# A graph network whose tables hold the layers' inputs instead of their products

## The chip, the cores and the metric

The kernel runs on one core of a Trainium2 chip. The metric is the time of the device for one execution, in microseconds (us). Before the change three runs took 3906.57, 3909.14 and 3911.62 us.

Five engines work side by side: TensorE (PE in the rows: matrix products, and turns, which are products with the identity), VectorE (DVE), ScalarE (ACT), GpSimd (POOL, which issues the indirect transfers) and SyncE (SP, which issues the plain ones).

## The reference

Four graph stages follow one another over 50,000 nodes of 128 features and 25,000 edges sorted by target, each as x = layernorm(x + stage(x)). The stage that matters here is the second, a graph convolution of three layers:

```python
deg = segment_sum(1, dst) + 1            # a loop at every node
norm = deg[src] ** -0.5 * deg[dst] ** -0.5
h = x @ W_in + b_in
for i in range(3):
    xw = h @ Ws[i]
    agg = segment_sum(xw[src] * norm, dst) + bs[i]
    h = relu(agg)
```

The stage ahead of it (attention with four heads, gelu, layernorm) gives x1; after it comes x2 = layernorm(x1 + h), then two more attention stages. A product with Ws[i] and the weighted sum over edges can be exchanged: sum of (h @ W) is (sum of h) @ W.

## The kernel before

The work is in stages, each a block in which every engine has its own written instruction list; semaphores order them, and all engines meet between the stages.

- *Node stage.* All nodes are computed as if they had no edge: 49 iterations over 1024 rows each (two halves of 512), with the layernorms of iteration t-1, t-2, t-5, t-6 and t-7 in one batch on VectorE (forty columns: big, half_y, hx, wx, then rs and nm). For a chunk m = t-3, TensorE turns x1 (into the PSUM banks T_A and T_B), makes h1 = W_in Ws0 applied to it (with the feature on the partition), and beside it the same product with the node on the partition (rows_times), which are the rows of the first table, xw0; the same again with Ws1 for h2 and table xw1, and with Ws2 for table xw2. VectorE adds the bias to xw0 (L793), ScalarE copies xw1 and xw2 out of PSUM (L658, L677, L689, L703), and VectorE reads the copy of xw2 for h3 (L741) and v (L746). SyncE stores the three tables, x2 and x3. Meanwhile GpSimd gathers x at the ends of the edges and writes a map of nodes that are targets.
- *First hop.* The attention stage for the targets of edges, 25 iterations of 1024 edge slots. VectorE forms the batch of scales up to nm (L1485), ScalarE normalises (L1377) and then normalises again to x1 (L1389); TensorE turns x1, ScalarE copies (L1363), TensorE multiplies by W_in Ws0 on top of a bias row (L1308, L1310), ScalarE scales the rows by deg^-0.5 (L1349), and SyncE stores them in the first table.
- *Graph layers 0, 1 and 2.* Each 49 chunks of 512 slots. GpSimd gathers four times 128 rows of the layer's table (L1607), up to six chunks ahead; SyncE loads the slots' own rows. TensorE turns both; VectorE first adds the bias times root(deg) to the own rows (L1709, four instructions), then runs a segmented sum over the gathered columns (the scan, L1714) and adds the own column (L1721, with_self). ScalarE applies relu (hT, L1653); TensorE multiplies by the next layer's matrix and ScalarE scales (L1661) to the rows of the next table. In layer 2 TensorE only turns hT back and VectorE makes v = x1 + deg^-0.5 h from PSUM (L1758, four instructions), followed by a layernorm. Beside them a part of the final layernorms of all nodes (y) and turns of the edge features run.
- *The last two hops* follow from 2585 us on; their order comes from a table of places. The change doesn't touch them.

## Time and profile before

| | |
|---|---|
| median of three runs | 3909.14 us |
| the profiled execution | 3892.84 us, span 3891.1 us |
| VectorE busy | 3381.2 us (87%) |
| TensorE busy | 2681.5 us (69%) |
| ScalarE busy | 2534.8 us (65%) |
| GpSimd busy | 2446.9 us (63%) |

The span is the time from the first to the last instruction in the profile. The shares are means over stages with different limits, so that each stage has to be read by itself. A busy time counts the union of an engine's instructions; on VectorE they overlap by about a tenth of a microsecond where nothing waits, so a duration and the distance of two starts are not the same. In brackets behind an instruction of a timeline stands how long the engine was idle ahead of it, and what ended that. The granted clock is TensorE's, as a share of 2.4 GHz; its low level is 1.2 GHz.

### The profile page before, as it was taken

What the parts mean: (1) busy time and instruction counts of PE and PEld (TensorE: products, weight loads), DVE (VectorE), ACT (ScalarE), POOL (GpSimd) and SP (SyncE); (2) the same over time, 40 slices, a digit from 0 to 9 for tenths busy, and PEclk for the clock granted to TensorE, in tenths of its full rate; (3) what the DMA queues carried; (4) which work ended last, traced back from release to release, by engine and by line L of the source; (5) the groups of instructions that cost most, each with busy time, mean ns of one, the idle gap of its engine ahead of it and who ended that gap; (6) DMA issues with size and microseconds to landing.
All of it is one profiled execution on the core that took longest, in us unless ns stands there. A gap on an engine that the chain in (4) does not pass through costs nothing. (4 is left out here: it accounts for less than half of the span.)

```text
span 3891.1 us, 48029 instructions
## 1 busy us (share of the span) xinstructions
PE 2681.5 (69%) x11826; PEld 1733.3 (45%) x11826; DVE 3381.2 (87%) x7569; ACT 2534.8 (65%) x5535; POOL 2446.9 (63%) x2202
## 2 busy tenths in 40 slices
PE   5877877778861688865656545547888885776774
PEld 4555555555540344435545534424444442444442
DVE  5999999999987788858868869969999996998886
ACT  3788788878862466645646646637777775565554
POOL 4565566666650566517767767757766651788777
PEclk9999999999985677767676775659999887666555
DMA  3888877766652988837868868832333221433332
GB/s 102 195 197 199 199 197 199 199 197 194 203 177 79 252 253 258 253 110 239 270 196 257 261 203 252 248 122 81 90 86 87 83 77 52 112 96 92 95 95 65
DMA packets 402066, 644.05 MB, mean 166 GB/s; under 512 B 127455, under 2 KB 207720, under 8 KB 401790
## 3 DMA queue, kind: packets, MB, share of 16 engines
q1 hardware_dynamic: 332030, 527.96, 45.1%
q0 software_dynamic: 69760, 113.02, 11.9%
q8 instruction: 99, 1.62, 0.2%
q14 instruction: 177, 1.45, 0.1%
HBM read 347.78 MB, written 296.81 MB: 166 GB/s over the span
## 5 line engine op out<-in xcount | busy, mean ns | idle before, releaser
L1607 POOL DMA_INDIRECT gs_g<-table_xw,slot_idx x588 | 612.2, 1041 | 297.7 <-issue 257.0
L898 POOL DMA_INDIRECT gs_t<-table_x,slot_idx x392 | 439.7, 1122 | 310.9 <-POOLq L83 125.4
L507 POOL DMA_INDIRECT gs<-x,src_idx x200 | 219.5, 1098 | 342.1 <-DMA xd_rows<-gd 249.3
L1274 POOL DMA_INDIRECT slot_idx<-node_map,src_idx x200 | 242.9, 1214 | 192.7 <-DMA slot_idx<-node_map,src_idx 91.7
L378 PE MATMUL ps<-ident,own_g 128*128 128x128 f32 x588 | 139.8, 382 | 251.5 <-DVE own_g L1709 251.2
L1653 ACT ACTIVATE hT_g<-u_g 128x512 f32<-128x512 f32 x147 | 92.5, 629 | 330.9 <-DVE u_g L1721 330.7
L507 POOL DMA_INDIRECT gd<-x,dst_idx x200 | 243.9, 1220 | 60.9 <-issue 59.1
L1883 POOL DMA_INDIRECT out<-x_t,end_idx x196 | 234.6, 1197 | 59.9 <-issue 59.0
L495 POOL DMA_INDIRECT node_map<-slot_no,end_idx x200 | 222.9, 1114 | 61.0 <-issue 60.6
L898 POOL DMA_INDIRECT own_t<-table_x,own_idx x196 | 222.2, 1134 | 59.7 <-issue 59.4
L1714 DVE TENSOR_TENSOR_SCAN agg_g<-same_seg,agg_g,ps 128x512 f32<-128x512 uint8 x147 | 187.3, 1274 | 48.5 <-PE ps L378 48.2
L1709 DVE SCALAR_TENSOR_TENSOR own_g<-bs_row,root,own_g 128x128 f32<-128x128 f32 x588 | 166.7, 345 | 67.5 <-DMA own_g<-table_xw 67.4
L378 PEld LDWEIGHTS ps<-ident,own_g 128*128 128x128 f32 x588 | 93.2, 192 | 290.8 <-DVE own_g L1709 290.5
L378 PE MATMUL ps<-ident,gs_g 128*128 128x128 f32 x588 | 130.6, 365 | 127.5 <-DMA gs_g<-table_xw,slot_idx 127.4
L611 ACT ACTIVATE x_b<-v_b,nm,rs 128x128 f32<-128x128 f32 x392 | 156.2, 480 | 68.8 <-DVE nm L785 68.8
L2000 ACT COPY xsT_t<-ps 128x512 f32<-128x512 f32 x98 | 56.4, 576 | 208.9 <-PE ps L378 208.9
L378 PE MATMUL ps<-ident,gs_t 128*128 128x128 f32 x392 | 81.4, 345 | 126.9 <-DMA gs_t<-table_x,slot_idx 99.7
L611 ACT ACTIVATE x_b<-s_b,nm,rs 128x128 f32<-128x128 f32 x392 | 156.3, 485 | 11.9 <-DVE nm L785 11.9
L378 PEld LDWEIGHTS ps<-ident,gs_g 128*128 128x128 f32 x588 | 99.2, 193 | 141.8 <-issue 88.9
L378 PEld LDWEIGHTS ps<-ident,gs_t 128*128 128x128 f32 x392 | 56.9, 176 | 236.4 <-issue 236.4
L384 PEld LDWEIGHTS ps<-WS,h1T 128*128 128x128 f32 x784 | 100.8, 194 | 137.4 <-DVE xw_b L793 112.3
L384 PE MATMUL ps<-WS,h1T 128*128 128x128 f32 x784 | 109.9, 284 | 74.4 <-DVE xw_b L793 74.4
(366 smaller groups left out, 9514.9 us busy)
## 6 DMA issues: line engine op xcount, KB each, us to landing
table_xw<-xw_b SPq DMA_DIRECT2D x147, 512.0 KB, 4.8
table_x<-x_b SPq DMA_DIRECT2D x98, 512.0 KB, 2.7
own_g<-table_xw SPq DMA_DIRECT2D x147, 256.0 KB, 4.3
x_in<-x SPq DMA_DIRECT2D x49, 512.0 KB
y_g<-table_x SPq DMA_DIRECT2D x49, 512.0 KB, 4.8
table_xw<-xw_g SPq DMA_DIRECT2D x98, 256.0 KB
out<-y_g SPq DMA_DIRECT2D x49, 512.0 KB, 3.6
pen_t<-pen_row SPq DMA_DIRECT2D x98, 256.0 KB, 4.0
```

The lines of the kernel that those rows point to most:

```text
L378: last = nc.tensor.transpose(to[0:width, j * P:(j + 1) * P], t[:, j * width:(j + 1) * width], ident[:])
L384: last = nc.tensor.matmul(to[:, j * D:(j + 1) * D], tT[:, j * P:(j + 1) * P], W[:], start=True, stop=bias_row is None)
L495: pool.indirect_dma_start(out=node_map, out_offset=bass.IndirectOffsetOnAxis(ap=end_idx[:, t:t + 1], axis=0), in_=slot_no[:, t:t + 1], in_ ...
L507: pool.indirect_dma_start(out=to[k % 3][:, j * D:(j + 1) * D], out_offset=None, in_=x, in_offset=bass.IndirectOffsetOnAxis(ap=of[:, n:n + ...
L611: last = nc.scalar.activation(to[:, k * D:(k + 1) * D], of(k), ACT.Identity, scale=r[:, n, k:k + 1], bias=b[:, n, k:k + 1])
L898: pool.indirect_dma_start(out=self.B[L % RING][g][:, t * D:(t + 1) * D], out_offset=None, in_=table, in_offset=bass.IndirectOffsetOnAxis(a ...
L1274: pool.indirect_dma_start(out=slot_idx[:, t:t + 1], out_offset=None, in_=node_map, in_offset=bass.IndirectOffsetOnAxis(ap=src_idx[:, t:t + ...
L1607: pool.indirect_dma_start(out=gs[c % 6][:, j * D:(j + 1) * D], out_offset=None, in_=tables[layer], in_offset=bass.IndirectOffsetOnAxis(ap= ...
L1653: nc.scalar.activation(hT[c % 3][:], u[c % 2][:], ACT.Relu).then_inc(S("hT"), 1)
L1709: V.scalar_tensor_tensor(out=blk, in0=bs_row[layer][:], scalar=root4[:, k:k + 1], in1=blk, op0=ALU.mult, op1=ALU.add).then_inc(S("own_bias ...
L1714: V.tensor_tensor_scan(agg[t % 3][:], same_seg[:, t * CH:(t + 1) * CH], T_X[t % 2], agg[(t - 1) % 3][:, CH - 1:CH], ALU.mult, ALU.add).the ...
L1883: pool.indirect_dma_start(out=out, out_offset=bass.IndirectOffsetOnAxis(ap=end_idx[:, k:k + 1], axis=0), in_=B[L % RING]["x4"][:, t * D:(t ...
```

## The change

The tables no longer hold products but the inputs of the layers: x1, h1 and h2 (with the factor deg^-0.5 for the edge slots), and each graph layer sums first and multiplies by its own matrix then. The order of a layer is: turn and scan, with_self, product with WS[layer] (z), bias times root(deg) added on VectorE (zb, four instructions, from PSUM), relu with the scale on ScalarE (h_e, four instructions), store. It runs one chunk deeper. In layer 2, v becomes one addition of 512 columns from SBUF, a chunk later than before.

The bias b_in Ws0 of the first layer is carried by x1 itself: x1 is a layernorm's output, whose features have the mean 0. Its shift nm is raised by 1.0 with one small VectorE instruction on 8 columns, so that the mean of x1 is 1; the matrix is centred (centre times W_in Ws0) and the bias, divided by 128, is added to each of its rows. The following layernorms take the constant out again.

In the node stage the row products with W_in Ws0 go, with VectorE's two bias additions; the row products with Ws1 become turns of h1, and turns of h2 are added, while the row products with Ws2 stay, for h3. VectorE reads h3 directly from PSUM, in two halves. In the first hop the turns of x1, their copies and the products go; the rows are x1 times deg^-0.5, by ScalarE, and the same small addition of 1.0 stands behind its nm. The diff below is cut; the second halves and the other waits read alike.

```diff
-    tables = [dram(f"table_{n}", [NT + rows, D]) for n, rows in (("xw0", ET), ("xw1", GT), ("xw2", GT), ("x2", GT), ("x3", GT))]
+    tables = [dram(f"table_{n}", [NT + rows, D]) for n, rows in (("x1", ET), ("h1", GT), ("h2", GT), ("x2", GT), ("x3", GT))]
...
+        pe.wait_ge(S("wi0"), 1)
+        pe.wait_ge(S("centre"), 1)
+        nc.tensor.matmul(ps[:, 4, 0:P], centre[:], WI[:], start=True, stop=True).then_inc(S("wi0_centred"), 1)
...
+        V.scalar_tensor_tensor(out=WS[0][:], in0=xw0_bias[:], scalar=1.0 / D, in1=ps[:, 4, 0:P], op0=ALU.mult, op1=ALU.add)
...
-                store(tables[0], xw_b[0], "xw0_out", 2, t - 3, "xw0", 2 * (t - 2))
-                store(tables[1], xw_b[1], "xw1_out", 2, t - 3, "xw1", 2 * (t - 2))
-            if live(t - 3):
-                store(tables[2], xw_b[2], "xw2_out", 2, t - 3, "xw2", 2 * (t - 2))
+                store(tables[0], x1_b, "x1_out", 3, t - 3, "b_out", 2 * (t - 2))
+                store(tables[1], h_b[1], "h1_out", 2, t - 3, "h1_rows", 2 * (t - 2))
+                store(tables[2], h_b[2], "h2_out", 2, t - 3, "h2_rows", 2 * (t - 2))
...
-                    pe.wait_ge(S("xw2"), 2 * c)
+                    pe.wait_ge(S("h3"), 2 * c)
                 turn(pe, T_A, half(x1_b[c % 3], 0)).then_inc(S("x1T_ps"), 1)
                 pe.wait_ge(S("b_out"), 2 * c + 2)
                 if c:
-                    pe.wait_ge(S("xw1"), 2 * c)
+                    pe.wait_ge(S("h2_rows"), 2 * c)
                 turn(pe, T_B, half(x1_b[c % 3], 1)).then_inc(S("x1T_ps"), 1)
                 pe.wait_ge(S("x1T"), 2 * c + 1)
-                nc.tensor.matmul(T_C, WI0[:], x1T[0][:], start=True, stop=True).then_inc(S("h1_ps"), 1)
-                rows_times(pe, T_D, x1T[0], WI0).then_inc(S("xw0_ps"), 1)
+                nc.tensor.matmul(T_C, WS[0][:], x1T[0][:], start=True, stop=True).then_inc(S("h1_ps"), 1)
...
             if m:
                 pe.wait_ge(S("h1T"), 2 * c + 1)
                 nc.tensor.matmul(T_C, WS[1][:], h1T[0][:], start=True, stop=True).then_inc(S("h2_ps"), 1)
-                pe.wait_ge(S("xw0"), 2 * c + 1)
-                rows_times(pe, T_D, h1T[0], WS[1]).then_inc(S("xw1_ps"), 1)
+                turn(pe, T_D, h1T[0]).then_inc(S("h1_turned"), 1)
...
                 pe.wait_ge(S("h2T"), 2 * c + 1)
                 rows_times(pe, T_C, h2T[0], WS[2]).then_inc(S("xw2_ps"), 1)
+                pe.wait_ge(S("h1_rows"), 2 * c + 1)
+                turn(pe, T_D, h2T[0]).then_inc(S("h2_turned"), 1)
             if f:
...
-                act.wait_ge(S("xw2_ps"), 2 * c + 1)
+                act.wait_ge(S("h2_turned"), 2 * c + 1)
                 if c >= 2:
-                    landed(act, "xw2_out", 2, c - 2)
-                    act.wait_ge(S("h3"), c - 1)
-                nc.scalar.copy(half(xw_b[2][c % 2], 0), T_C).then_inc(S("xw2"), 1)
+                    landed(act, "h2_out", 2, c - 2)
+                nc.scalar.copy(half(h_b[2][c % 2], 0), T_D).then_inc(S("h2_rows"), 1)
...
-                v.wait_ge(S("xw2"), 2 * (cv + 1))
-                V.tensor_tensor(wide_rows(h3_b[:]), wide_rows(xw_b[2][cv % 2][:]), row_of_all(bs_row[2]), ALU.add).then_inc(S("h3"), 1)
-            if live(cv):
-                v.wait_ge(S("h3"), cv + 1)
+                for h in range(2):
+                    v.wait_ge(S("xw2_ps"), 2 * cv + h + 1)
+                    V.tensor_tensor(rows4(half(h3_b, h)), rows4((T_C, T_A)[h]), each_row(bs_row[2]), ALU.add).then_inc(S("h3"), 1)
+                v.wait_ge(S("h3"), 2 * (cv + 1))
...
             v.wait_ge(S("batch"), n0 + 10)
-            V.scalar_tensor_tensor(out=b, in0=of[:, :, 1], scalar=-1.0, in1=r, op0=ALU.mult, op1=ALU.mult).then_inc(S("scaled"), 1)
-
-            m, c, a = live(t - 3), t - 3, t - 1
+            V.scalar_tensor_tensor(out=b, in0=of[:, :, 1], scalar=-1.0, in1=r, op0=ALU.mult, op1=ALU.mult).then_inc(S("batch"), 1)
+            v.wait_ge(S("batch"), n0 + 11)
+            V.tensor_scalar(nm[t % 2][:, LNB, :], nm[t % 2][:, LNB, :], 1.0, None, ALU.add).then_inc(S("scaled"), 1)
+
+            a = t - 1
             for h in range(2):
-                if m:
-                    v.wait_ge(S("xw0_ps"), 2 * c + h + 1)
-                    if h == 0 and c >= 2:
-                        landed(v, "xw0_out", 2, c - 2)
-                    V.tensor_tensor(rows4(half(xw_b[0][c % 2], h)), rows4((T_D, T_B)[h]), each_row(xw0_bias), ALU.add).then_inc(S("xw0"), 1)
                 if live(a):
                     v.wait_ge(S("scaled"), t + 1)
                     v.wait_ge(S("w"), a + 1)
...
-        def xw_rows(c, h):
-            pe.wait_ge(S("x1T"), 2 * c + h + 1)
-            pe.wait_ge(S("xw"), 2 * c + h)
-            nc.tensor.matmul(T_W, ones[:], bias_row4[:], start=True, stop=False, skip_group_check=True)
-            for j in range(SUB):
-                last = nc.tensor.matmul(T_W[:, j * D:(j + 1) * D], x1T[h][:, j * P:(j + 1) * P], WI0[:],
-                                        start=False, stop=j == SUB - 1, skip_group_check=True)
-            last.then_inc(S("xw_ps"), 1)
...
         def scaled_rows(c, h):
-            act.wait_ge(S("xw_ps"), 2 * c + h + 1)
+            act.wait_ge(S("x1"), 2 * c + h + 1)
             if h == 0 and c >= 3:
-                landed(act, "xw_out", 3, c - 3)
+                landed(act, "xs_out", 3, c - 3)
             for j in range(SUB):
                 k = (2 * c + h) * SUB + j
-                last = nc.scalar.activation(blocks(xw_b[c % 3])(4 * h + j), blocks(T_W)(j), ACT.Copy, scale=dis4[:, k:k + 1])
-            last.then_inc(S("xw"), 1)
+                last = nc.scalar.activation(blocks(xs_b[c % 3])(4 * h + j), blocks(x1_b[c % 3])(4 * h + j), ACT.Copy, scale=dis4[:, k:k + 1])
+            last.then_inc(S("xs"), 1)
...
-                    pe.wait_ge(S("own_bias"), SUB * (t + 1))
+                    landed(pe, "own_in", 4, t)
...
-                    pe.wait_ge(S("hT"), c + 1)
-                    if last_layer:
-                        if c >= 2:
-                            pe.wait_ge(S("v"), c - 1)
-                        turn(pe, T_W[c % 2], hT[c % 3]).then_inc(S("h_ps"), 1)
-                    else:
-                        if c >= 2:
-                            pe.wait_ge(S("xw"), c - 1)
-                        rows_times(pe, T_W[c % 2], hT[c % 3], WS[layer + 1]).then_inc(S("xw_ps"), 1)
+                    pe.wait_ge(S("with_self"), c + 1)
+                    if c >= 2:
+                        pe.wait_ge(S("zb"), SUB * (c - 1))
+                    rows_times(pe, T_Z[c % 2], u[c % 3], WS[layer]).then_inc(S("z_ps"), 1)

         @block.scalar
         def _(act):
             for t in range(G_CH + 8):
-                c = t - 1
+                c = t - 3
                 if live(c):
-                    act.wait_ge(S("with_self"), c + 1)
-                    if c >= 3:
-                        act.wait_ge(S("h_ps" if last_layer else "xw_ps"), c - 2)
-                    nc.scalar.activation(hT[c % 3][:], u[c % 2][:], ACT.Relu).then_inc(S("hT"), 1)
-                c = t - 3
-                if live(c) and not last_layer:
-                    act.wait_ge(S("xw_ps"), c + 1)
-                    if c >= 3:
+                    act.wait_ge(S("zb"), SUB * (c + 1))
+                    if last_layer:
+                        if c >= 3:
+                            act.wait_ge(S("v"), c - 2)
+                    elif c >= 3:
                         landed(act, "stored", 3, c - 3)
+                    scale = dis4 if last_layer else inv4
                     for j in range(SUB):
                         k = c * SUB + j
-                        last = nc.scalar.activation(xw[c % 3][:, j * D:(j + 1) * D], T_W[c % 2][:, j * D:(j + 1) * D], ACT.Copy,
-                                                    scale=inv4[:, k:k + 1])
-                    last.then_inc(S("xw"), 1)
+                        last = nc.scalar.activation(h_e[c % 3][:, j * D:(j + 1) * D], zb[c % 3][:, j * D:(j + 1) * D], ACT.Relu,
+                                                    scale=scale[:, k:k + 1])
+                    last.then_inc(S("h_rows"), 1)
...
-                    landed(v, "own_in", 4, t)
-                    for j in range(SUB):
-                        k = t * SUB + j
-                        blk = own[t % 4][:, j * D:(j + 1) * D]
-                        V.scalar_tensor_tensor(out=blk, in0=bs_row[layer][:], scalar=root4[:, k:k + 1], in1=blk,
-                                               op0=ALU.mult, op1=ALU.add).then_inc(S("own_bias"), 1)
                     v.wait_ge(S("xsT_ps"), t + 1)
                     if t:
                         v.wait_ge(S("agg"), t)
...
                 if live(c):
                     v.wait_ge(S("own_ps"), c + 1)
                     v.wait_ge(S("agg"), c + 1)
-                    if c >= 2:
-                        v.wait_ge(S("hT"), c - 1)
-                    V.tensor_tensor(rows4(u[c % 2][:]), agg[c % 3].rearrange("f (p j) -> f j p", j=SUB), rows4(T_O[c % 2]), ALU.add).then_inc(S("with_self"), 1)
+                    if c >= 3:
+                        v.wait_ge(S("z_ps"), c - 2)
+                    V.tensor_tensor(rows4(u[c % 3][:]), agg[c % 3].rearrange("f (p j) -> f j p", j=SUB), rows4(T_O[c % 2]), ALU.add).then_inc(S("with_self"), 1)
+                c = t - 3
+                if live(c):
+                    v.wait_ge(S("z_ps"), c + 1)
+                    if c >= 3:
+                        v.wait_ge(S("h_rows"), c - 2)
+                    for j in range(SUB):
+                        k = c * SUB + j
+                        V.scalar_tensor_tensor(out=zb[c % 3][:, j * D:(j + 1) * D], in0=bs_row[layer][:], scalar=root4[:, k:k + 1],
+                                               in1=T_Z[c % 2][:, j * D:(j + 1) * D], op0=ALU.mult, op1=ALU.add).then_inc(S("zb"), 1)
...
+                    v.wait_ge(S("h_rows"), q + 1)
+                    landed(v, "x1_in", 8, q)
+                    if q >= 3:
+                        v.wait_ge(S("x2"), q - 2)
+                    V.tensor_tensor(v_b[q % 3][:], h_e[q % 3][:], x1_e[q % 8][:], ALU.add).then_inc(S("v"), 1)
...
-                    for j in range(SUB):
-                        k = q * SUB + j
-                        last = V.scalar_tensor_tensor(out=v_b[q % 3][:, j * D:(j + 1) * D], in0=T_W[q % 2][:, j * D:(j + 1) * D], scalar=dis4[:, k:k + 1],
-                                                      in1=x1_e[q % 8][:, j * D:(j + 1) * D], op0=ALU.mult, op1=ALU.add)
-                    last.then_inc(S("v"), 1)
...
```

In one iteration of the node stage VectorE has, from the layernorms' shift nm to the multiplications by gamma (a_b) and what follows, and then ahead of v in the next iteration, before:

```order
L785 SCALAR_TENSOR_TENSOR nm<-raw,rs 128x40
L793 TENSOR_TENSOR xw_b<-ps,xw_bias 128x512
L797 TENSOR_TENSOR a_b<-ps,gamma 128x512
L800 SCALAR_TENSOR_TENSOR t_b<-a_b,rs,t_b 128x128 x4
L793 TENSOR_TENSOR xw_b<-ps,xw_bias 128x512
L797 TENSOR_TENSOR a_b<-ps,gamma 128x512
...
L737 SCALAR_TENSOR_TENSOR t_b<-x_in,beta 128x1024
L741 TENSOR_TENSOR h_b<-xw_b,bs_row 128x1024
L746 SCALAR_TENSOR_TENSOR v_b<-h_b,x_b 128x1024
```

And now (the names without numbers: h_b is h3_b, xw_b above is the rows of table xw0):

```order
L787 SCALAR_TENSOR_TENSOR nm<-raw,rs 128x40
L789 TENSOR_SCALAR nm<-nm 128x8
L796 TENSOR_TENSOR a_b<-ps,gamma 128x512
L799 SCALAR_TENSOR_TENSOR t_b<-a_b,rs,t_b 128x128 x4
L796 TENSOR_TENSOR a_b<-ps,gamma 128x512
...
L739 SCALAR_TENSOR_TENSOR t_b<-x_in,beta 128x1024
L744 TENSOR_TENSOR h_b<-ps,bs_row 128x512 x2
L748 SCALAR_TENSOR_TENSOR v_b<-h_b,x_b 128x1024
```

Two additions of 512 columns have gone, one small addition has come, and h3 is two halves from PSUM instead of one wide instruction from SBUF.

TensorE in the node stage, from its last product of h2 to the first product with Ws1, before:

```order
L384 MATMUL ps<-WS,h2T 128x128 x4
L378 MATMUL ps<-ident,x_in 128x128 x4
L378 MATMUL ps<-ident,x_b 128x128 x8
L559 MATMUL ps<-x1T,WI 128x512
L384 MATMUL ps<-WI,x1T 128x128 x4
L530 MATMUL ps<-xT,W 128x512
L565 MATMUL ps<-x1T,WI 128x512
L384 MATMUL ps<-WI,x1T 128x128 x4
L378 MATMUL ps<-ident,x_in 128x128 x4
L571 MATMUL ps<-h1T,WS 128x512
L384 MATMUL ps<-WS,h1T 128x128 x4
```

And now:

```order
L387 MATMUL ps<-WS,h2T 128x128 x4
L381 MATMUL ps<-ident,h2T 128x128 x4
L381 MATMUL ps<-ident,x_in 128x128 x4
L381 MATMUL ps<-ident,x_b 128x128 x8
L561 MATMUL ps<-x1T,WI 128x512
L532 MATMUL ps<-xT,W 128x512
L566 MATMUL ps<-x1T,WI 128x512
L381 MATMUL ps<-ident,x_in 128x128 x4
L571 MATMUL ps<-h1T,WS 128x512
L381 MATMUL ps<-ident,h1T 128x128 x4
```

The row products between the turns and h1, h2 have gone; turns of h1 and h2 stand where products with Ws1 stood or where nothing was. The turn of x1 (x_b) waits for h3 now, and for ScalarE's copy of xw2 before.

VectorE in layer 2, one chunk (agg is the scan, u is with_self), before:

```order
L1709 SCALAR_TENSOR_TENSOR own_g_3<-bs_row,root,own_g_3 128x128 x4
L1714 SCALAR_TENSOR_TENSOR agg_g_1<-same_seg,agg_g_0,ps 128x512
L1721 TENSOR_TENSOR u_g_0<-agg_g_0,ps 128x512
L1745 BN_STATS st_g_0<-v_b_g_0 128x6 x2
L1749 RECIPROCAL rs_g_2<-sd_g_2 128x4
L1758 SCALAR_TENSOR_TENSOR v_b_g_1<-ps,dis,x_e_g_0 128x128 x4
L1765 SCALAR_TENSOR_TENSOR nm_g_2<-st_g_2,rs_g_2 128x4
```

And now:

```order
L1667 SCALAR_TENSOR_TENSOR agg_g_1<-same_seg,agg_g_0,ps 128x512
L1674 TENSOR_TENSOR u_g_0<-agg_g_0,ps 128x512
L1682 SCALAR_TENSOR_TENSOR zb_g_1<-bs_row,root,ps 128x128 x4
L1709 TENSOR_TENSOR v_b_g_0<-h_e_g_0,x_e_g_7 128x512
L1713 RECIPROCAL rs_g_1<-sd_g_1 128x4
L1718 BN_STATS st_g_2<-v_b_g_2 128x6 x2
L1723 SCALAR_TENSOR_TENSOR nm_g_1<-st_g_1,rs_g_1 128x4
```

The four additions to the own rows stood ahead of the scan; four of the same shape now stand behind it, and the four of v are one.

## Rows read from the trace of the kernel before

**Rows 1.** Stages (from:to, length, busy time by engine, TensorE clock, DMA share, GB/s).

```profile
26.00:1204.00 1178.00, 912.05 (x5108) 617.79 (x5108) 1113.36 (x2884) 916.17 (x2014) 686.34 (x600) 0.97 0.69 188
...
1263.00:1726.00 463.00, 352.72 (x1100) 193.11 (x1100) 358.89 (x848) 289.19 (x726) 242.90 (x200) 0.74 0.78 227
...
2292.00:2582.00 290.00, 138.50 (x652) 116.21 (x652) 268.33 (x736) 157.93 (x373) 203.66 (x196) 0.61 0.73 224
```

**Rows 2.** Timeline of VectorE, node stage (start, us, engine, line, op, names).

```profile
298.95 1.22 DVE L741 TENSOR_TENSOR h_b<-xw_b,bs_row 128x1024 f32<-128x1024 f32 x1
...
305.26 0.19 DVE L785 SCALAR_TENSOR_TENSOR nm<-raw,rs 128x40 f32<-128x40 f32 x1
...
305.97 0.67 DVE L797 TENSOR_TENSOR a_b<-ps,gamma 128x512 f32<-128x512 f32 x1
306.68 1.14 DVE L800 SCALAR_TENSOR_TENSOR t_b<-a_b,rs,t_b 128x128 f32<-128x128 f32 x4
307.74 0.69 DVE L793 TENSOR_TENSOR xw_b<-ps,xw_bias 128x512 f32<-128x512 f32 x1
308.33 0.69 DVE L797 TENSOR_TENSOR a_b<-ps,gamma 128x512 f32<-128x512 f32 x1
...
321.65 1.22 DVE L741 TENSOR_TENSOR h_b<-xw_b,bs_row 128x1024 f32<-128x1024 f32 x1
322.91 1.25 DVE L746 SCALAR_TENSOR_TENSOR v_b<-h_b,x_b 128x1024 f32<-128x1024 f32 x1
```

**Rows 3.** Timeline of ScalarE, the same iteration.

```profile
303.68 0.58 ACT L617 COPY xT<-ps 128x512 f32<-128x512 f32 x1 [0.64 <-PE ps L378]
305.48 3.19 ACT L611 ACTIVATE x_b<-v_b,nm,rs 128x128 f32<-128x128 f32 x8 [1.22 <-DVE nm L785]
...
314.79 3.21 ACT L611 ACTIVATE x_b<-t_b,nm,rs 128x128 f32<-128x128 f32 x8
```

**Rows 4.** Timeline of TensorE, the same iteration.

```profile
306.10 1.16 PE L384 MATMUL ps<-WS,h1T 128*128 128x128 f32 x8 [1.60 <-DVE xw_b L793]
...
320.01 1.06 PE L378 MATMUL ps<-ident,x_b 128*128 128x128 f32 x8 [0.30 <-ACT xw_b L703]
```

**Rows 5.** Timeline of the first hop, one of its last full iterations.

```profile
1683.06 0.17 DVE L1482 SCALAR_TENSOR_TENSOR rs_h<-hx_h,half_y_h 128x16 f32<-128x16 f32 x1
1683.27 0.17 DVE L1485 SCALAR_TENSOR_TENSOR nm_h<-raw_h,rs_h 128x16 f32<-128x16 f32 x1
1683.48 2.90 ACT L1377 ACTIVATE n_b_h<-ps,nm_h,rs_h 128x128 f32<-128x128 f32 x8 [1.88 <-DVE nm_h L1485]
1685.01 0.69 DVE L1490 TENSOR_TENSOR n_b_h<-n_b_h,gamma 128x512 f32<-128x512 f32 x1 [1.57 <-ACT n_b_h L1377]
...
1685.12 1.10 PE L1336 MATMUL ps<-ident,gT_h 128*128 128x128 f32 x4 [3.46 <-ACT n_b_h L1377]
```

**Rows 6.** Timeline of the first hop's end, ScalarE.

```profile
1707.38 3.19 ACT L1389 ACTIVATE x_b_h<-t_b_h,nm_h,rs_h 128x128 f32<-128x128 f32 x8
...
1722.97 1.14 ACT L1349 ACTIVATE xw_b_h<-ps,dis 128x128 f32<-128x128 f32 x4 [4.22 <-PE ps L1310]
```

**Rows 7.** GpSimd's gathers of layers 0 and 2 (min/median/max ns, first and last start).

```profile
L1607 POOL DMA_INDIRECT gs_g<-table_xw,slot_idx x196: 992/997/1955, 1729.5 to 1993.1; - x196
...
L1607 POOL DMA_INDIRECT gs_g<-table_xw,slot_idx x196: 992/997/1981, 2292.4 to 2554.5; - x196
```

**Rows 8.** Timeline of VectorE at the end of layers 0 and 2.

```profile
1998.95 1.27 DVE L1714 TENSOR_TENSOR_SCAN agg_g<-same_seg,agg_g,ps 128x512 f32<-128x512 uint8 x1
...
2543.03 1.27 DVE L1714 TENSOR_TENSOR_SCAN agg_g<-same_seg,agg_g,ps 128x512 f32<-128x512 uint8 x1
...
2545.95 1.08 DVE L1758 SCALAR_TENSOR_TENSOR v_b_g<-ps,dis,x_e_g 128x128 f32<-128x128 f32 x4
...
2548.08 1.26 DVE L1714 TENSOR_TENSOR_SCAN agg_g<-same_seg,agg_g,ps 128x512 f32<-128x512 uint8 x1
...
2563.17 1.27 DVE L1714 TENSOR_TENSOR_SCAN agg_g<-same_seg,agg_g,ps 128x512 f32<-128x512 uint8 x1
```

129 lines of the change are left out of this document (51 added, 78 removed).

## The prediction

> **What bounds the kernel now.** I read the busy time by stage first [rows 1]. Only two of the stages that the change touches have a full engine. In the node stage (26 to 1204 us) VectorE is busy 1113 of 1178 us; its filling and its tail are in that, and between them it never rests. One iteration takes 321.65 - 298.95 = 22.70 us [rows 2]. The graph layers are paced by GpSimd: the first and the last of a layer's 196 gather instructions start 1993.1 - 1729.5 = 263.6 us apart in layer 0 and 262.1 us in layer 2, although their VectorE work differs [rows 7]; that is 1.35 us an instruction and 5.4 us for a chunk of four. VectorE is busy 268 of 290 us in layer 2 [rows 1], and level with GpSimd there. The first hop (1263 to 1726 us) has no full engine; what closes its loop is VectorE's batch, then eight normalising instructions on ScalarE, for the first half of which VectorE waits 1.57 us [rows 5]. The last two hops (2585 us on) are not touched.
>
> **Node stage, per iteration.** Two bias additions from PSUM go (L793). Their duration is 0.68 us, but VectorE starts the next instruction 308.33 - 307.74 = 0.59 us after one where nothing waits, and 306.68 - 305.97 = 0.71 us after one whose result is waited for [rows 2]. I count by starts. The second L793 frees 0.59. Around the first, nm (L785) to the multiplication by gamma (L797) takes 305.97 - 305.26 = 0.71 now; with the chain of nm, the new add of 1.0 on 128x8, and the multiplication waiting for it, it takes two small dependent steps of 1683.27 - 1683.06 = 0.21 [rows 5], so 0.42: 0.29 freed. The h3 addition (L741), 1024 wide from SBUF and 322.91 - 321.65 = 1.26 from start to start [rows 2], becomes two halves from PSUM: 0.59 and 0.71, 1.30: 0.04 lost. The new small add is not in the trace; its bounds are nothing extra (hidden in the pipeline, 0.10 less) and twice the small step (0.21 more), and I take one step. Net 0.59 + 0.29 - 0.04 = 0.84 us per iteration, for 49 iterations 41 us; in the eight iterations without this work only the small add is left, with about 0.3 us each, 2 us. Node stage: -39 us. If the durations counted in full, it would be 2 x 0.68 - (2 x 0.68 - 1.22) - 0.17 = 1.05 us, 51 us: that is the upper end.
>
> VectorE: DVE Perf Modes, of the Trainium skill (section The DRAIN you can't avoid), says that the next operation starts only when the pipe is empty and that a semaphore between two costs nothing extra. The rows differ: 0.59 us without a wait and 0.71 with one [rows 2]. By the page both would count alike and the gain would be the 51 us; I go by the rows.
>
> What TensorE and ScalarE get. ScalarE's instructions keep their number and shape. TensorE drops the two row products with W_in, has four turns by the identity where two row products with Ws1 stood, and so has less to do. But one wait moves. T_A and T_C are now read by VectorE's h3 and not by ScalarE's copy, so TensorE's first turn of x1 (now at 320.01, just before VectorE's iteration begins) can start only after w and both h3 halves. So there is a loop: ScalarE's last normalising of x1 (b_out), VectorE's w, h3, TensorE's turn, x1T, h1, gelu, copy of xT, ScalarE's three normalisings, b_out. I measure it from the start of h3 (L741, 298.95 in one iteration). Both halves of h3 end at 1.3. From the turn of x1 to the end of the second copy of xT it is now 303.68 + 0.58 + 22.70 - 320.01 = 6.95 us [rows 2 to 4]; without the two products with W_in (eight records take 1.16 us with their start-up [rows 4]; in a pipeline that is already full I estimate 0.9) 5.2. ScalarE is thus free at 6.5 and gets VectorE's scales at 305.48 - 298.95 + 0.25 = 6.8, so the scales still decide. b_out ends at 314.79 + 3.21 - 298.95 + 0.25 = 19.3 [rows 3]. The next w, as wide as L741, starts some 1.2 us ahead of the next h3 and so wants it at 21.86 - 1.2 = 20.7. The loop has 1.4 us of slack: VectorE stays the bound, with an iteration of 22.70 - 0.84 = 21.86 us. The cover of that edit is thin; if it is gone, every us more on this loop is 49 us.
>
> **First hop.** The x1 turns, the bias rows, the products and the x1T copies go. TensorE is idle 3.46 us ahead of L1336 and nobody waits for it in the loop; ScalarE, which loses two copies, starts its normalisings the moment nm is there [rows 5]. What was removed lay beside the loop and gives nothing. What is added lies in it: one more small step of 0.21 us between nm and ScalarE, 25 times: +5 us. The tail is different. There, after the last x1 (1707.38 + 3.19 = 1710.57), two turns, two copies and two products run one after the other until the last scaled rows end at 1722.97 + 1.14 = 1724.11 [rows 6]. Now 12 scaling instructions follow x1 at once. By the spacing of ScalarE's instructions from PSUM (2.90 / 8 = 0.36) or from SBUF (3.19 / 8 = 0.40) [rows 5, 6] that is 4.3 to 4.8 us after an x1 that itself ends about 3 us sooner, since the two waits for products ahead of it are gone: about 1712, 12 us sooner (9 if x1 ends no sooner, 13 if it ends 4 us sooner). First hop: -7 us.
>
> **Graph layers.** Layers 0 and 1: VectorE's four own_bias and four zb have the same shape; a PSUM operand is new, and the nearest row has one too: four of v_b in 1.08 us [rows 8], about as the four of own_bias, so nothing is added. ScalarE loses the 128x512 relu. GpSimd's gathers pace both as before, so nothing comes back. The pipeline is a stage deeper at the end (product, zb, relu, store after the last chunk, where relu, product, scale stood): +0.5 us each, bounds -1 and +5 (one chunk period). Layer 2: v goes from four instructions (1.08 us) to one 128x512 addition (0.6 to 0.7, by the starts in [rows 2]), and VectorE's chunk from 2548.08 - 2543.03 = 5.05 us to some 4.6 [rows 8]. It cannot outrun the gathers. But its last scan starts 2563.17 - 2554.5 = 8.7 us after the last gather, in layer 0 1998.95 - 1993.1 = 5.9 [rows 7, 8]: this lag of 2.8 us goes, and the deeper pipeline costs at the end about what the shorter iterations there give: -3 us, bounds -8 and +4. TensorE has a real product there where it had a turn, but it waited for VectorE's own_bias, a wait that goes.
>
> **Sum.** Node -39, first hop -7, layers 0 and 1 +1, layer 2 -3, set-up (one product and one addition more) +0.5: -47 us. The profiled execution took 3892.84 us with a span of 3891.1; it becomes about 3846. It was 16.3 us under the median of the three runs, 3909.14, so the same step from the median gives 3862.
>
> **Rivals.**
> - *The loop through ScalarE and TensorE takes over because TensorE's clock falls (slower).* The node stage is granted 0.97 of the full clock, its longest regular idle times of TensorE being 1.60 us [rows 1, 4]; the first hop, with 3.46 us ones, is granted 0.74 [rows 1, 5]. The new order packs TensorE's early work and leaves it idle for about 2 us before the turn of g's second half (it then waits for gelu) and 1.6 us before the turn of x1. If these bring the level to 1.2 GHz, the loop's turns and products (two turns, three wide products, about 3.6 us [rows 4]) take twice as long. b_out then ends at 22.9 instead of 19.3, and an iteration lasts about 22.9 + 1.2 = 24.1 us: 49 x 1.4 = +69 us, less 8 elsewhere, 3970 us. It decides from where the loop exceeds 22.70 us, that is from 2.2 us more on it, a low clock in over half of that stretch. Against it: TensorE's share of busy time falls little (turns replace products), and its idle times stay far below those of the first hop. TensorE: Matmul & The Clock Gate, of the Trainium skill (Part 1), says that idleness, not load, brings the low level; that is this rival's mechanism, and whether idle times of 2 us suffice no row of this trace shows. Chance 0.07.
> - *The slack of the loop is overestimated at full clock*, or the layers pay a chunk period each for the deeper pipeline. With 0.5 us more per iteration (22.4) the node stage gives 13 us and not 39: 3888; with 5 us in each of three layers, 3877. For it: 1.4 us of slack from a dozen terms. Against: nearly all of them are rows. Chance 0.13 to the two, for a total of 3874 to 3900.
> - *The removed instructions count with their full duration* (the 51 us) and layer 2 gives 8: 3909 - 51 - 7 - 6 = 3845. Chance 0.12.
> - *The work goes but nothing moves*, as in the first hop's loop: VectorE would have to have been waiting in the node stage, where the busy time [rows 1] leaves room only for the filling and the tail. Result 3909 - 8 = 3901 or above. Chance 0.03.
>
> **From this to the numbers.** My forecast, 3862 with a range of its own of 3848 to 3874, has 0.65. Range for 8 in 10: 3842 to 3892, from the full durations to most of the second rival. A difference of 0.2%, 7.8 us, is about what a measurement tells from none. Faster by more are the forecast, the full durations and the second rival, together 0.90, of which I take 0.03 for what no case names: 0.87. Same: the last rival's 0.03 and a little of that, 0.04. Slower: 0.07 and the rest, 0.09.
>
> **What would show it.** Right: VectorE's node iteration at 21.8 to 22.0 us with no idle time before w, h3 or hd; TensorE's clock near 1.0 there; first hop's iteration 0.2 us longer and its end 12 us shorter; the gathers of each layer 262 to 264 us as before; layer 2 ending about 3 us closer behind its last gather. Wrong: VectorE waiting for ScalarE ahead of w or hd in the node stage, a granted clock below 0.9 there, or a layer whose gathers wait for TensorE.

## The result, and the profile after

The changed kernel takes 3859.4 us against 3907.9 (medians of four runs each): a ratio of 0.9877, 95% interval 0.9856 to 0.9899. A second series gave 3844.6 against 3893.8 (medians of four and seven runs), 0.9873 (0.9856 to 0.9890). The prediction was 3862 from 3909, 47 us; measured are 48.5 and 49.2.

First the stages of the kernel after (columns as in [rows 1]): node stage, first hop, layer 2.

```profile
26.00:1163.00 1137.00, 884.06 (x4324) 561.78 (x4324) 1071.32 (x2889) 912.90 (x2012) 672.33 (x600) 0.90 0.70 195
1222.00:1676.00 454.00, 206.33 (x400) 84.86 (x400) 363.41 (x876) 268.40 (x676) 240.05 (x200) 0.64 0.78 232
2238.00:2532.00 294.00, 160.16 (x848) 145.28 (x848) 246.76 (x588) 186.53 (x520) 206.16 (x196) 0.68 0.73 222
```

VectorE still fills the node stage. But the granted clock there is 0.90 where it was 0.97, and in the first hop 0.64 where it was 0.74. Next VectorE's timeline in the node stage, to hold against [rows 2]:

```profile
287.52 1.22 DVE L739 SCALAR_TENSOR_TENSOR t_b<-x_in,beta 128x1024 f32<-128x1024 f32 x1
288.66 1.28 DVE L744 TENSOR_TENSOR h_b<-ps,bs_row 128x512 f32<-128x512 f32 x2
289.97 1.23 DVE L748 SCALAR_TENSOR_TENSOR v_b<-h_b,x_b 128x1024 f32<-128x1024 f32 x1
...
295.02 0.20 DVE L787 SCALAR_TENSOR_TENSOR nm<-raw,rs 128x40 f32<-128x40 f32 x1
295.26 0.17 DVE L789 TENSOR_SCALAR nm<-nm 128x8 f32<-128x8 f32 x1
295.46 0.69 DVE L796 TENSOR_TENSOR a_b<-ps,gamma 128x512 f32<-128x512 f32 x1
296.19 1.14 DVE L799 SCALAR_TENSOR_TENSOR t_b<-a_b,rs,t_b 128x128 f32<-128x128 f32 x4
297.25 0.68 DVE L796 TENSOR_TENSOR a_b<-ps,gamma 128x512 f32<-128x512 f32 x1
...
309.42 1.22 DVE L739 SCALAR_TENSOR_TENSOR t_b<-x_in,beta 128x1024 f32<-128x1024 f32 x1
```

One iteration is 309.42 - 287.52 = 21.90 us (forecast 21.86). The halves of h3 take 289.97 - 288.66 = 1.31 from start to start, nm to the multiplication by gamma 0.44. The same timeline further on, at three successive w:

```profile
375.31 1.22 DVE L739 SCALAR_TENSOR_TENSOR t_b<-x_in,beta 128x1024 f32<-128x1024 f32 x1
376.44 1.28 DVE L744 TENSOR_TENSOR h_b<-ps,bs_row 128x512 f32<-128x512 f32 x2
...
397.11 0.19 DVE L734 TENSOR_SCALAR big<-raw 128x40 f32<-128x40 f32 x1
397.41 1.22 DVE L739 SCALAR_TENSOR_TENSOR t_b<-x_in,beta 128x1024 f32<-128x1024 f32 x1
398.56 1.28 DVE L744 TENSOR_TENSOR h_b<-ps,bs_row 128x512 f32<-128x512 f32 x2
...
419.33 1.22 DVE L739 SCALAR_TENSOR_TENSOR t_b<-x_in,beta 128x1024 f32<-128x1024 f32 x1
```

These are 22.10 and 21.92 us apart: at 397.41 w started 0.30 us behind big (L734) instead of 0.11. It had waited for b_out. Why, TensorE's timeline of the two iterations shows:

```profile
377.87 1.06 PE L381 MATMUL ps<-ident,x_b 128*128 128x128 f32 x8 [2.30 <-DVE h_b L744]
379.17 1.88 PE L561 MATMUL ps<-x1T,WI 128*128 128x512 f32 x2 [0.24 <-ACT x1T L633]
380.84 1.92 PE L532 MATMUL ps<-xT,W 128*128 128x512 f32 x2
...
399.98 1.06 PE L381 MATMUL ps<-ident,x_b 128*128 128x128 f32 x8 [0.25 <-DVE h_b L744]
401.29 1.12 PE L561 MATMUL ps<-x1T,WI 128*128 128x512 f32 x2 [0.24 <-ACT x1T L633]
402.25 1.02 PE L532 MATMUL ps<-xT,W 128*128 128x512 f32 x2
```

In the first iteration TensorE stood idle for 2.30 us ahead of the turn of x1, and the products behind it took 1.88 and 1.92 us, those of the next iteration 1.12 and 1.02: the 1.2 GHz level (from 379.45 to 382.80 us the granted clock is 0.50) against 2.4. ScalarE's chain passes through them. Its first normalising starts 384.80 - 376.44 = 8.4 us behind h3 and not 405.37 - 398.56 = 6.8, and its x1 follows:

```profile
384.80 3.19 ACT L613 ACTIVATE x_b<-v_b,nm,rs 128x128 f32<-128x128 f32 x8
...
394.10 3.21 ACT L613 ACTIVATE x_b<-t_b,nm,rs 128x128 f32<-128x128 f32 x8
...
405.37 3.19 ACT L613 ACTIVATE x_b<-v_b,nm,rs 128x128 f32<-128x128 f32 x8
...
414.68 3.21 ACT L613 ACTIVATE x_b<-t_b,nm,rs 128x128 f32<-128x128 f32 x8
```

b_out ended 0.10 us ahead of w in the slow iteration (397.31, 397.41) and 1.44 ahead in the fast one (417.89, 419.33). An early b_out makes TensorE idle, the clock falls, the next b_out is late, TensorE does not idle, the clock is back. Over 42 such iterations (133.4 to 1056.6) the mean is 21.98 us; before it is 22.74, where 22.70 is the shortest.

The first hop (VectorE, ScalarE; against [rows 5, 6]):

```profile
1610.92 0.17 DVE L1449 SCALAR_TENSOR_TENSOR nm_h<-raw_h,rs_h 128x16 f32<-128x16 f32 x1
1611.13 0.17 DVE L1451 TENSOR_SCALAR nm_h<-nm_h 128x8 f32<-128x8 f32 x1
```

```profile
1611.34 2.90 ACT L1342 ACTIVATE n_b_h<-ps,nm_h,rs_h 128x128 f32<-128x128 f32 x8 [2.09 <-DVE nm_h L1451]
...
1669.12 3.59 ACT L1320 ACTIVATE xs_b_h<-x_b_h,dis 128x128 f32<-128x128 f32 x12
```

The added 1.0 takes its step of 0.21 ahead of ScalarE, and the scans come 16.81 us apart (before 16.61). From the last scan to the last instruction it takes 1672.71 - 1636.92 = 35.8 us, before 1724.11 - 1675.63 = 48.5. Of these 12.7 us, 2.7 are x1's own end; the twelve scaling instructions behind it take 3.59 us where the forecast had 4.3 to 4.8.

Layer 2: GpSimd's gathers, VectorE's last scan, ScalarE's last normalising (against [rows 7, 8]).

```profile
L1573 POOL DMA_INDIRECT gs_g<-table_h,slot_idx x196: 993/1000/2058, 2238.0 to 2502.6; - x196
```

```profile
2507.04 1.28 DVE L1667 TENSOR_TENSOR_SCAN agg_g<-same_seg,agg_g,ps 128x512 f32<-128x512 uint8 x1 [0.56 <-PE ps L381]
```

```profile
2527.34 3.17 ACT L1653 ACTIVATE x_e_g<-v_b_g,nm_g,rs_g 128x128 f32<-128x128 f32 x8
```

The last scan starts 4.4 us behind the last gather (before 8.7), but the end is 23.5 us behind that scan (before 18.0). In that stretch v waits for ScalarE's normalising, for example:

```profile
2517.09 0.69 DVE L1709 TENSOR_TENSOR v_b_g<-h_e_g,x_e_g 128x512 f32<-128x512 f32 x1 [0.91 <-ACT x_e_g L1653]
...
2523.95 0.69 DVE L1709 TENSOR_TENSOR v_b_g<-h_e_g,x_e_g 128x512 f32<-128x512 f32 x1 [1.94 <-ACT x_e_g L1653]
```

Where the time went, profile against profile: VectorE's node stage ends 40.1 us earlier (the last of nm, before and after):

```profile
1203.51 0.21 DVE L785 SCALAR_TENSOR_TENSOR nm<-raw,rs 128x40 f32<-128x40 f32 x1
```

```profile
1163.40 0.17 DVE L789 TENSOR_SCALAR nm<-nm 128x8 f32<-128x8 f32 x1
```

The first hop from first scan to last instruction is 10.9 us shorter, layers 0 to 2 are -3.2, +0.3 and +3.8, and the two last hops, which are not touched, took 1317.7 us against 1305.6. The rest is 0.6 us less. The experiments are about which of these are the change's.

### The profile page after: what moved, and what is told of

Read it like the earlier page. It is cut to its first block and busy times, and to the rows that moved or that the text cites. A ratio compares the mean times of both kernels' runs of the same rounds, so it can differ in the third digit from the quotient of the medians.

```text
span 3852.5 us, 45264 instructions
## 1 busy us (share of the span) xinstructions
PE 2521.8 (65%) x10538; PEld 1591.5 (41%) x10538; DVE 3318.9 (86%) x7458; ACT 2505.0 (65%) x5534; POOL 2443.5 (63%) x2202
## 3 DMA queue, kind: packets, MB, share of 16 engines
q8 instruction: 88, 1.44, 0.2%
## 5 line engine op out<-in xcount | busy, mean ns | idle before, releaser
L897 POOL DMA_INDIRECT gs_t<-table_x,slot_idx x392 | 448.9, 1145 | 308.7 <-POOLq L83 125.7
L1573 POOL DMA_INDIRECT gs_g<-table_h,slot_idx x392 | 409.9, 1046 | 153.3 <-issue 116.7
L1620 ACT ACTIVATE h_e_g<-zb_g,inv 128x128 f32<-128x128 f32 x392 | 124.6, 389 | 270.0 <-DVE zb_g L1682 269.9
L1573 POOL DMA_INDIRECT gs_g<-table_x,slot_idx x196 | 203.0, 1036 | 152.8 <-issue 151.0
L509 POOL DMA_INDIRECT gd<-x,dst_idx x200 | 230.1, 1151 | 60.9 <-issue 59.7
L381 PEld LDWEIGHTS ps<-ident,gs_g 128*128 128x128 f32 x588 | 87.0, 183 | 380.3 <-issue 273.5
L387 PE MATMUL ps<-centre,gT 128*128 128x128 f32 x784 | 134.8, 326 | 111.6 <-ACT gT L623 96.8
L387 PEld LDWEIGHTS ps<-centre,gT 128*128 128x128 f32 x784 | 116.3, 228 | 130.9 <-ACT gT L623 110.7
L1287 PE MATMUL ps<-xsT_h,W 128*128 128x512 f32 x100 | 92.8, 1084 | 114.1 <-DVE a_b_h L1399 90.2
L1682 DVE SCALAR_TENSOR_TENSOR zb_g<-bs_row,root,ps 128x128 f32<-128x128 f32 x588 | 163.5, 341 | 1.1 <-PE ps L387 1.1
```

The costliest lines, as they stand in the source:

```text
L381: last = nc.tensor.transpose(to[0:width, j * P:(j + 1) * P], t[:, j * width:(j + 1) * width], ident[:])
L387: last = nc.tensor.matmul(to[:, j * D:(j + 1) * D], tT[:, j * P:(j + 1) * P], W[:], start=True, stop=bias_row is None)
L509: pool.indirect_dma_start(out=to[k % 3][:, j * D:(j + 1) * D], out_offset=None, in_=x, in_offset=bass.IndirectOffsetOnAxis(ap=of[:, n:n + ...
L897: pool.indirect_dma_start(out=self.B[L % RING][g][:, t * D:(t + 1) * D], out_offset=None, in_=table, in_offset=bass.IndirectOffsetOnAxis(a ...
L1573: pool.indirect_dma_start(out=gs[c % 6][:, j * D:(j + 1) * D], out_offset=None, in_=tables[layer], in_offset=bass.IndirectOffsetOnAxis(ap= ...
L1620: last = nc.scalar.activation(h_e[c % 3][:, j * D:(j + 1) * D], zb[c % 3][:, j * D:(j + 1) * D], ACT.Relu, scale=scale[:, k:k + 1])
```

## The experiments

The experiments ran on four chips: one had before_again, after_again, mix_hop1 and mix_layers, a second scalar2, scalar4, products and vector_add, a third the first run of add_off, best and filler, a fourth add_off_2. On the second and third every kernel was slower: before took 4148 and 4170 us there, layer 0's gathers 290 to 292 us against 259 to 265, and single node iterations lasted up to 36 us. The expectations call this late transfers; no run shows the cause. The kernel after wasn't run on these two, so no total that was expected against it was tested. In their own series the seven are: scalar2 4131.4, scalar4 4130.2, vector_add 4138.0 and products 4157.4 us, of which products is slower than before (ratio 1.0037, 1.0005 to 1.0069); add_off 4115.0, best 4132.3 and filler 4146.4 us. These totals don't follow the node iterations: scalar4's quiet ones add up to 28 us more than scalar2's, and its total is no longer. What stands across chips is the length of undisturbed iterations, which repeats to 0.05 us.

**before_again, after_again**: both kernels unchanged.

> The kernel before, unchanged, profiled a second time. In the two profiles at hand the last two hops, in which no instruction is changed, take 1305.6 us before (from 2585.5 on) and 1317.7 us after (from 2534.8 on), and layer 2 takes 293.0 and 296.8 us. Theory: both differences are scatter from one execution to the next; then this profile has last hops anywhere between 1300 and 1325 us and a layer 2 of 290 to 297 us. Rival: the change slows the last hops (another place of the tables, say); then they stay within 2 us of 1305.6 here and within 2 us of 1317.7 in the repeated kernel after. Node stage 1177 to 1178 us in either case.

> The kernel after, unchanged. Theory (scatter): last hops 1300 to 1325 us, the node stage's VectorE iteration 21.90 us and its end 40 us earlier than before's, the first hop 10.9 us shorter; the stages that the change touches give 50 us, so the ratio of medians is 0.987. Rival (the last hops are slower because of the change): last hops 1316 to 1320 us and a ratio nearer to 0.990.

Medians 3893.8 (seven runs of before; this one 3895.0) and 3844.6. Node stage: last nm at 1203.8 and 1162.1. Last hops 1303.5 and 1308.4 us: most of the 1317.7 was scatter, and the ratio stayed. First hop 451.2 and 444.1 us; without its first iteration, which took 17.8 to 21.4 us in the profiles of either kernel, 431.9 and 423.0, and 430.7 and 422.8 in the first pair: 8 us are the change's, the other 3 were scatter. That the last hops pay nothing is not shown: all five profiles with the new node stage on chips without late transfers have 1305.8 to 1317.7 us, the two of before 1303.5 and 1305.6.

**mix_hop1**: the first hop of before in the kernel after.

```
-        <first hop of after>
+    WI0, xw0_bias = WS[0], bs_row[0]
+        <first hop of before>
```

> The kernel after with the first hop of before (its turns of x1, bias rows, products and x1T copies are back, the added 1.0 is gone; the scaled products go into the table where the scaled inputs stood, so the layers compute with other numbers). Theory: what went out of the loop lay beside it, the added 1.0 costs its 0.2 us in the loop, the tail gives 12 and the start 3. So the first hop's scans come 16.61 us apart here against 16.81, and its end is 10 to 12 us later: total 11 us above the kernel after. Rival: the removed work gave something in the loop, which the added step hides; then the scans are more than 16.7 us apart and the total is over 15 us above.

Median 3854.25 (ratio 0.9895, 0.9878 to 0.9912), 9.7 us above after. VectorE's scans are 16.62 us apart:

```profile
1603.16 2.35 DVE L1442 TENSOR_TENSOR_SCAN num_h<-nst_h,num_h,a_b_h 128x1024 f32<-128x1024 f32 x1
1619.78 2.35 DVE L1442 TENSOR_TENSOR_SCAN num_h<-nst_h,num_h,a_b_h 128x1024 f32<-128x1024 f32 x1
```

All that left the loop was covered, the added step costs its 0.2, and the end is again 48.5 us behind the last scan. The start gives nothing (first iteration 21.0 us here).

**mix_layers**: the three graph layers of before in the kernel after.

```
-    for layer in range(3):   <layers of after>
+    for layer in range(3):   <layers of before>
```

> The kernel after with the three graph layers of before (own_bias on VectorE, relu on ScalarE ahead of the product, turn and four additions in layer 2; so the layers compute with other numbers). My prediction was that the new layers give 2 us in sum, with layer 2 giving 3; the profile at hand has layers 0, 1 and 2 at -3.2, +0.3 and +3.8 us. Theory now: the layers are paced by the gathers and differ by scatter only in the gathers' 261 to 265 us; what the change does is in layer 2's end, where the lag of the last scan behind the last gather falls by 4.3 us and the stretch from the last scan to the last instruction grows by 5.5. So the total is within 3 us of the kernel after. Rival: the new layer 2 is really 4 us slower; then this one is 3 to 6 us faster than after.

Median 3850.2 (0.9889, 0.9872 to 0.9905), 5.6 us above after, with intervals that overlap. Layers 280.9, 283.8 and 292.6 us. With the two profiles of before, the old layer 2 has 293.0, 293.8, 292.6; the new one 296.8, 295.0, 296.2 and 295.7 (after twice, mix_hop1, add_off_2): 2.8 us slower. That is +2.1 in the gathers (261.8 to 263.9 on average), -4.7 in the lag of the last scan (9.0 to 4.3), +5.5 from there to the end (18.0 to 23.5). Old layer 0 has 282.1 on average and the new one 278.8, old layer 1 282.4 and the new one 280.7, both with a scatter of 2 to 5 us. The rival's mechanism (layer 2 slower) holds, its total doesn't; nor is the total within the theory's 3 us. In layers 0 and 1 the stretch from the last scan to the end, where the deeper pipeline should cost 0.5 us each, has grown from 8.9 to 9.3 and from 8.1 to 9.2 us.

**vector_add**: what a VectorE instruction that waits for nothing costs.

```
+    if h == 1:
+        V.tensor_tensor(rows4(half(a_b2, h)), rows4(T_G[h]), each_row(gamma0), ALU.add)
     V.tensor_tensor(rows4(half(a_b, h)), rows4(T_G[h]), each_row(gamma0), ALU.mult)
```

> The kernel after with one addition of 128x512 from PSUM back on VectorE in each of the 49 iterations (between the first t_b and the second a_b; it waits for nothing and nobody reads it). Theory, by starts: 0.59 us each, iteration 22.49, total 29 us above after. Rival, by full durations: 0.69, iteration 22.59, total 34. Rival (VectorE is not the bound any more after the change): under 0.3 us an iteration, total under 15.

Undisturbed iterations take 22.50 us, 0.59 more than 21.91. VectorE's timeline shows the start of the next instruction inside the added one's duration:

```profile
917.81 0.69 DVE L798 TENSOR_TENSOR a_b<-ps,gamma 128x512 f32<-128x512 f32 x1
918.41 0.68 DVE L799 TENSOR_TENSOR a_b<-ps,gamma 128x512 f32<-128x512 f32 x1
```

So starts count, not durations. VectorE: DVE Perf Modes, of the Trainium skill (section The DRAIN you can't avoid), has the next operation start only when the pipe is empty, which would be 0.69; it adds that one that is not held starts earlier, a half that the prediction left out, and with that half the 0.59 agrees.

**scalar2, scalar4**: the slack of the loop through ScalarE and TensorE.

```
     nc.scalar.activation(h1T[1][:], T_A, ACT.Relu, bias=h1_bias[:, 0:1])
+    for k in range(2):                       # 4 in scalar4
+        nc.scalar.copy(spare[k][:], x1T[1][:])
```

> The kernel after with two more copies of 128x512 on ScalarE in each node iteration that has the graph part (49 of 57), put behind the second gelu-free h1T, that is inside the loop w, h3, turn of x1, ScalarE, b_out; nobody reads what they write. A copy takes 0.47 to 0.48 us from start to start when nothing waits, so the loop gets 0.95 us longer. My prediction gave the loop 1.4 us of slack; the profile after has b_out ending at 307.97 and w starting at 309.42, the same 1.4. Theory: VectorE's iteration stays at 21.90 us and the total within 3 us of after. Rival (the slack is under 1 us): the iteration grows, to 22.2 or more, and the total by 15 us or more.

> The same with four copies, 1.9 us more in the loop. Theory (1.4 us of slack): VectorE now waits for ScalarE ahead of w, the iteration grows by about 0.5 us to 22.4, the total by 20 to 30 us. Rival (ScalarE's other idle time takes the copies up, slack over 2 us): no change. Rival (slack under 1 us): iteration 22.8 or more, the total 45 us or more above after.

Undisturbed iterations: 21.91 with two copies, 22.49 with four. VectorE's w of scalar4:

```profile
689.74 1.23 DVE L742 SCALAR_TENSOR_TENSOR t_b<-x_in,beta 128x1024 f32<-128x1024 f32 x1 [0.34 <-ACT x_b L614]
712.23 1.23 DVE L742 SCALAR_TENSOR_TENSOR t_b<-x_in,beta 128x1024 f32<-128x1024 f32 x1 [0.35 <-ACT x_b L614]
```

The four copies take 2.07 us there, so the loop without them is 20.42 and its slack at full clock 21.91 - 20.42 = 1.49: the forecast's 1.4 holds, at full clock.

**products**: TensorE's two row products with W_in back.

```
     nc.tensor.matmul(T_C, WS[0][:], x1T[0][:], start=True, stop=True)
+    rows_times(pe, T_D, x1T[0], WS[0])
...
     nc.tensor.matmul(T_A, WS[0][:], x1T[1][:], start=True, stop=True)
+    rows_times(pe, T_B, x1T[1], WS[0])
```

> The kernel after with the two row products of x1 with W_in back on TensorE in the node stage (eight instructions of 128x128 behind each product that gives h1; nobody reads them; the additions that VectorE made on them stay away). Theory: TensorE's work was hidden, the gain of 0.8 us an iteration is VectorE's alone; with 0.9 us more on the loop it is still inside its slack of 1.4 us, so the iteration stays at 21.90 and the total within 3 us of after. The granted clock of the node stage, 0.90 after against 0.97 before, goes back to 0.95 or more if it is TensorE's idle time that lowered it. Rival: removing TensorE's work was part of the gain, and the iteration is 22.2 or more. Second rival for the clock: the turns by the identity lower it, and it stays at 0.90.

Undisturbed iterations take 22.07 us, not 21.90, with w behind b_out by 0.11 each time:

```profile
957.16 1.12 PE L561 MATMUL ps<-x1T,WI 128*128 128x512 f32 x2 [0.24 <-ACT x1T L635]
958.12 1.05 PE L387 MATMUL ps<-WI,x1T 128*128 128x128 f32 x8
959.01 1.02 PE L532 MATMUL ps<-xT,W 128*128 128x512 f32 x2
959.87 1.02 PE L567 MATMUL ps<-x1T,WI 128*128 128x512 f32 x2
960.73 1.05 PE L387 MATMUL ps<-WI,x1T 128*128 128x128 f32 x8
```

The two stand one behind the other in the loop, 0.89 and 0.89 us by starts, and 20.4 + 1.8 is 22.2, near the 22.07. This expectation counted one of them, the prediction's own step (6.95 to 5.2 us) both. So taking them out was a condition for a part of the gain: with them 0.16 us of each iteration's 0.8 is lost, less than the rival's 0.3. In its quiet stretch (900 to 1000 us) the clock is 0.97 with the turns by the identity still there, so the second rival fails.

**filler**: is it the idle time ahead of x1's turn that lowers the clock?

```
+    pe.wait_ge(S("h2_rows"), 2 * c - 1)
+    for _ in range(2):
+        turn(pe, T_D, half(x1_b[c % 3], 0))
     pe.wait_ge(S("h3"), 2 * c)
```

> The kernel after with two more turns of x1 (four 128x128 each, nobody reads them) on TensorE ahead of its wait for h3, in the idle time of 2.30 us that stands in every second iteration ahead of the turn of x1. Theory: this idle time lets TensorE's clock fall, the products behind it take 1.88 and 1.92 us instead of 1.12 and 1.02, and the loop needs all of its slack, 0.2 us over, in that iteration. Filled up to 1.4 us, the clock of 200 to 1000 us goes from 0.91 to 0.97 or more, the first product of h1 always takes 1.12, b_out ends 1.4 us ahead of w every time, and the iterations are all 21.90; total 2 to 4 us less than after. Rival: the clock falls at the idle time ahead of g's second half (2.0 to 2.5 us) alone, or for the kind of instruction; then clock and pattern stay, and the two turns make the iteration longer.

The stage as a whole was disturbed (clock 0.91 with idle times of other kinds), so its mean decides nothing. Its quiet iterations do, for example:

```profile
597.98 1.04 PE L381 MATMUL ps<-ident,x_b 128*128 128x128 f32 x8
600.39 1.09 PE L381 MATMUL ps<-ident,x_b 128*128 128x128 f32 x8 [1.37 <-DVE h_b L747]
601.72 1.12 PE L564 MATMUL ps<-x1T,WI 128*128 128x512 f32 x2 [0.24 <-ACT x1T L636]
602.68 1.02 PE L532 MATMUL ps<-xT,W 128*128 128x512 f32 x2
```

1.37 us idle where 2.30 stood, and 1.12 where 1.88 stood. In all 13 iterations of up to 22.12 us between 200 and 1100 us these products take 1.12 or 1.13, while the idle time ahead of g's second half is still 1.8 to 2.5 us: the rival, that this one alone slows them, fails. After's own rows say the same: from 300 to 1050 us, all 11 turns of x1 behind 2.29 to 2.34 us of idle time are followed by products of 1.87 to 2.08 us, all 15 behind 0.24 to 0.74 by 1.12 or 1.13, and the 8 in between (1.57 to 1.80) by either. That filling gives the 2 to 4 us of the expectation isn't shown.

**add_off, best, add_off_2**: the added step out of the way.

```
     V.scalar_tensor_tensor(out=b, ...)                       # nm, then_inc batch
-    v.wait_ge(S("batch"), n0 + 11)
-    V.tensor_scalar(nm[t % 2][:, LNB, :], ..., 1.0, None, ALU.add).then_inc(S("scaled"), 1)
+    if live(a):
+        v.wait_ge(S("w"), a + 1)
+        for h in range(2):
+            V.tensor_tensor(rows4(half(a_b, h)), rows4(T_G[h]), each_row(gamma0), ALU.mult).then_inc(S("ag"), 1)
+    v.wait_ge(S("batch"), n0 + 11)
+    V.tensor_scalar(nm[t % 2][:, LNB, :], ..., 1.0, None, ALU.add).then_inc(S("scaled"), 1)
     for h in range(2):                                       # the eight t_b
...
-    act.wait_ge(S("scaled"), t + 1)
+    act.wait_ge(S("batch"), 11 * (t + 1))
...
+    act.wait_ge(S("scaled"), t + 1)
     for h in range(2):
         apply(LNB, ...)
```

> The kernel after with the same arithmetic in another order: both multiplications by gamma (a_b) go directly behind nm, the added 1.0 behind them, then the eight t_b; ScalarE waits for nm, and for the added 1.0 only ahead of the normalising that needs it; the same in the first hop, where the added 1.0 then falls into time in which VectorE waits for ScalarE anyway. Theory: in the node stage the added step costs 0.24 us and each wait of t_b for a_b 0.12 to 0.14; all three go, the iteration is 21.4 us instead of 21.9, and 49 of them give 25 us. In the first hop the scans are 16.60 us apart instead of 16.81, 5 us. Total 30 us less than after. Rival (ScalarE and TensorE's loop is already the bound in the iterations in which w waits for b_out): the loop of 22.1 us in every second iteration stays, and the gain in the node stage is under 12 us.

best adds this order of VectorE's last third, and layer 2's v earlier:

```
-    stats of t_b; hd_b; stats of hd_b; stats of g; d_b; eight s_b; stats of s_b; stats of g
+    d_b; stats of t_b; hd_b; eight s_b; stats of hd_b; stats of s_b; stats of g
...
-    q = t - 4                        # v, ahead of the statistics
+    q = t - 3                        # v, last in VectorE's iteration; statistics, root and normalising one t earlier
```

> add_off and two more changes of order. In the node stage VectorE's last third is interleaved so that none of its instructions follows directly the one whose result it reads (d_b, stats of t_b, hd_b, s_b, stats of hd_b, stats of s_b, stats of g): four starts of 0.1 us less, the iteration 21.0 us. In layer 2 v goes to the end of VectorE's iteration t-3 and its statistics, root, and normalising one iteration earlier, as deep as the pipeline was before the change. Theory: by the loop of ScalarE and TensorE at full clock (20.5 us) the iteration can reach 21.0, and with a shorter slack TensorE's idle time ahead of the turn of x1 falls below the 1.6 us that before had at a clock of 1.00, so the clock of the node stage goes back to 0.97 or more. Layer 2: last scan to end 18 us instead of 23.5, the layer 4 us shorter. Total 54 us less than after. Rival: TensorE stays at the low level in every second iteration, the loop of 22.1 decides, and it gives under 25 us.

> add_off again, since in its first run transfers of the node stage came late, for the kernel before as well (4170 us against 3894), and covered the total; its undisturbed iterations took 21.39 us. Theory: where transfers come in time, VectorE's iterations take 21.39 us, some of them 22.0 where TensorE's clock has fallen ahead of the turn of x1 (the loop then decides), with a mean of 21.5 to 21.7 against 21.97 for the kernel after; the first hop is 6 us shorter. Total 19 to 29 us less than after, that is a ratio to before of 0.980 to 0.983 where after has 0.987. Rival: the low level comes in every second iteration and the mean is 21.8; then 12 us, 0.984 or more. If transfers are late again, only the undisturbed iterations tell, 21.39 us as before.

add_off_2 ran on one of the faster chips: 3821.6 us against 3898.5, a ratio of 0.9806 (0.9788 to 0.9824), the fastest version here. VectorE's timeline:

```profile
443.95 0.20 DVE L788 SCALAR_TENSOR_TENSOR nm<-raw,rs 128x40 f32<-128x40 f32 x1
444.06 1.28 DVE L794 TENSOR_TENSOR a_b<-ps,gamma 128x512 f32<-128x512 f32 x2
445.26 0.16 DVE L796 TENSOR_SCALAR nm<-nm 128x8 f32<-128x8 f32 x1
445.33 2.19 DVE L801 SCALAR_TENSOR_TENSOR t_b<-a_b,rs,t_b 128x128 f32<-128x128 f32 x8
...
479.94 1.23 DVE L740 SCALAR_TENSOR_TENSOR t_b<-x_in,beta 128x1024 f32<-128x1024 f32 x1 [0.36 <-ACT x_b L613]
```

nm to a_b is 0.11 instead of 0.44, and the added step takes 0.07. The node stage ends 16 us earlier than after_again's (1146.5) and the first hop is 6 us shorter (438.2). Two iterations of 21.40 are followed by one of 22.1 in which w waits for b_out (behind idle times of 1.91 to 1.94 us TensorE is at the low level, behind 1.21 to 1.26 at the full one), a mean of 21.63 over the 39 from 176.8 to 1020.2 us. The first hop's scans are 16.60 apart. The first run of add_off had 21.39 in quiet iterations, best 20.91 (forecast 21.0). best's layer 2 ended 19.7 us behind its last scan (forecast 18), so v and its statistics one step earlier give back 3.8 of the 5.5 us. But in best's disturbed node stage w waited for b_out by up to 1.9 us time and again, the clock was 0.88 there (forecast 0.97), and its total, 4132 us against add_off's 4115 in the same series, is no gain; whether it is one on a faster chip wasn't tried.

## Why the prediction was right, point by point

- **Node stage, -39: measured -40.1 and -41.7.** 22.70 to 21.90 us by VectorE's rows: -0.59 for the second addition (vector_add shows that price), -0.27 for the first with the added step (forecast -0.29), +0.05 for h3 (0.04). The added step costs the 0.2 us that I took, not nothing. The closeness is partly luck: averaged over the 42 iterations from the seventh w to the last the gain is 0.76 us and not the forecast's 0.84, 32 us in all, and the filling and the tail give the other 8, where the forecast took the eight iterations without graph work to lose 2.
- **The loop's slack.** Right at full clock: ScalarE's normalisings start 405.37 - 398.56 = 6.8 us behind h3 and b_out ends at 19.3, both as forecast, and scalar4 has 1.49 us of slack for the 1.4. What the step left out is the clock, and there the first rival's mechanism is real. TensorE idles 2.3 us ahead of x1's turn (forecast 1.6), and falls to the low level behind it. Its price was 1.5 us on b_out in that iteration (20.9 us behind h3 for 19.3), the slack and a little more, so only 0.1 to 0.2 us reach VectorE, in about every third iteration: some 3 us of the stage. I gave that rival 0.07 as an all-or-nothing case, with 24.1 us; the trace shows why it can't be one here: only two of the wide products ran slow (the turns ahead of them kept their 1.06 us, the third product took 1.16), and a late b_out removes the idle time that caused it. Two signs that I named for being right failed by this, no idle time before w and a clock near 1.0 (it is 0.90), and one for being wrong, VectorE waiting for ScalarE ahead of w, came true at that small price. TensorE: Matmul & The Clock Gate, of the Trainium skill (Part 1), has idleness as the cause, and these rows agree.
- **First hop, -7: measured -8**, +5 in the loop (24 x 0.2) and -12.7 at the end (forecast -12). The 10.9 of the first pair of profiles holds 3 us of scatter.
- **Layers 0 and 1, +1: measured about -5**, the means of three and four profiles each with a scatter as large; their gathers pace them as forecast, and the deeper pipeline costs 0.4 and 1.1 us at their ends (forecast 0.5 each).
- **Layer 2, -3: measured +2.8**, inside its bounds (-8 to +4), wrong in sign. The step that failed is "the deeper pipeline costs at the end about what the shorter iterations there give". It costs 5.5 us: each chunk still to be finished passes once more between VectorE and ScalarE, and v waits for the normalising that frees its buffer (the idle times of 0.91 and 1.94 us above). best, which keeps the hand-over and moves v and its statistics, has 3.8 us of it back, so most of the cost is v's place and its waits. The lag gave more than forecast, 4.7 and not 2.8. That the gathers themselves take 2.1 us more is not explained.
- **Sum.** -40, -8, -5, +3 and -0.5 are -50.5; medians fell by 48.5 and 49.2. The last hops took 6 us more on average in the profiles with the new node stage, which would leave -44; whether that is scatter or a cost stays open. The total within 2 us of the forecast owes something to luck: layers 0 and 1 and layer 2 missed by 6 us each, in opposite directions.

## What to carry to other kernels

Price an instruction of a full engine by the distance of starts, with a wait and without, and put small dependent steps behind independent wide ones: here that order was worth another 22 us by the stages (27 by the ratios to before, 0.9873 and 0.9806). Slack of a loop is a number at one clock: work taken off TensorE makes it idle, and the slower clock can eat the slack that the removal made. A stage that is paced by its gathers still ends by its pipeline's depth, which no busy time shows: a step more cost 0.4 and 1.1 us at the end of layers 0 and 1, and 5.5 in layer 2, where v stood a chunk later and waited for a buffer.

## What the runs showed of the hardware that was not expected

- The clock swings from one iteration to the next without costing more than 0.2 us: 0.84 and 1.00 in successive iterations of 21.9 us in the kernel after.
- An idle TensorE of 1.21 to 1.26 us left the clock at full level, one of 1.91 us or more ahead of the same turns did not, in the 39 iterations of add_off_2 from 200 to 1030 us. The idle time ahead of the turns doesn't decide alone: in three quiet iterations of vector_add it was 2.05 to 2.07 us, and the products behind still took 1.12 or 1.13.
- Two of the four chips of the experiments took 4148 and 4170 us for the kernel before, where the others took 3894 and 3898, with the gathers of a layer 28 us longer and single node iterations of up to 36 us. A gain of VectorE is partly covered there: add_off had 0.9881 against before on the second of these and 0.9806 on a faster chip.
